# One gathered tile of field 23 in each quad, fetched row by row from ScalarE's queue

## The reference

```python
emb = jax.vmap(lambda tbl, idx: tbl[idx], in_axes=(0, 1), out_axes=1)(embed_tables, sparse)   # [2048, 26, 32]
bi = emb[:, FIRST, :] * emb[:, SECOND, :]                      # the 325 pairs of fields
a = jax.nn.relu(jnp.einsum('bpd,dh->bph', bi, att_w_w) + att_w_b)
scores = jnp.einsum('bph,ho->bpo', a, att_d_w) + att_d_b
att_weight = jax.nn.softmax(scores, axis=1)
att_out = jnp.sum(att_weight * bi, axis=1)
x = jnp.concatenate([att_out, dense], axis=-1)
out = jax.nn.sigmoid(x @ fin_w + fin_b)
```

## Time and profile before

| | |
|---|---|
| median of three runs | 483.76 us |
| the profiled execution | 483.39 us |
| its span, first to last instruction | 481.6 us |
| TensorE matmuls, busy | 450.2 us (93%) |
| VectorE, busy | 372.6 us (77%) |
| GpSimd, busy | 347.9 us (72%) |
| ScalarE, busy | 95.8 us (20%) |

### The profile page before, as it was taken

One profiled execution on the slowest core, in us unless ns is written; L12 is line 12 of the kernel. 1 busy time (PEld: TensorE's weight loads), 2 busy tenths in 40 slices (PEclk: granted clock), 3 DMA queues, 4 the chain that ended last, 5 costly groups with the idle time before them and its releaser, 6 DMA issues.

```text
span 481.6 us, 6198 instructions
## 1 busy us (share of the span) xinstructions
PE 450.2 (93%) x2280; PEld 177.6 (37%) x2280; DVE 372.6 (77%) x645; ACT 95.8 (20%) x198; POOL 347.9 (72%) x372
## 2 busy tenths in 40 slices
PE   0699999999998999999999899999999899999884
PEld 0354443343333533333333443333334344333221
DVE  6337788796965979799775969879786788887985
ACT  0000101131252011112243101113234201114253
POOL 5777777777777777777777777777777777777740
PEclk9999999999999999999999999999999999999998
DMA  6933743121122223222112222213111222322210
GB/s 221 250 13 15 147 58 36 13 15 13 15 13 15 14 14 79 15 14 14 14 14 13 15 13 15 13 13 15 14 13 16 14 15 13 15 13 14 15 10 1
DMA packets 13661, 15.06 MB, mean 31 GB/s; under 512 B 6368, under 2 KB 12608, under 8 KB 13248
## 3 DMA queue, kind: packets, MB, share of 16 engines
q0 software_dynamic: 11776, 6.05, 23.1%
q1 hardware_dynamic: 1360, 7.53, 4.2%
q10 hardware_dynamic: 496, 1.09, 0.6%
HBM read 14.61 MB, written 0.03 MB: 30 GB/s over the span
## 4 chain that ended last, share of the span: by engine, by line
PE 78%; POOL 8%; DVE 5%; issue 4%; DMA 3%; ACT 1%; POOLq 0%; DVEq 0%
PE looked_own L391 33%; PE back_s L391 16%; PE first L405 13%; PE sums_f L415 12%; POOL emb L368 8%; PE sums_s L429 3%; DVE onehot L667 2%; DMA chunk_numbers<-index_chunk 1%; DMA emb<-tables,rows 1%; DMA chunk_of<-chunk_numbers 1%; PE back_f L442 1%; PE back_s L452 1%; DVE look_masked L678 1%; DMA par<-params 1%; DVE ring L691 0%
## 5 line engine op out<-in xcount | busy, mean ns | idle before, releaser
L368 POOL DMA_INDIRECT emb<-tables,rows x324 | 305.9, 944 | 98.7 <-issue 96.9
L691 DVE TENSOR_TENSOR ring<-emb_t,turned 128x512 f32<-128x512 f32 (+9 forms) x180 | 193.9, 1114 | 3.4
L391 PE MATMUL looked_own<-look_table,onehot 128*128 128x448 f32 x434 | 178.0, 554 | 17.0 <-DVE onehot L667 16.7
L391 PEld LDWEIGHTS looked_own<-look_table,onehot 128*128 128x128 f32 x434 | 79.5, 192 | 114.4 <-issue 114.4
L507 ACT ACTIVATE hidden<-first,par 128x512 f32<-128x512 f32 (+1 forms) x84 | 56.5, 678 | 284.7 <-PE first L405 284.4
L391 PE MATMUL back_s<-look_table,onehot 128*128 128x448 f32 x238 | 94.4, 545 | 3.1 <-DVE score L739 3.1
L405 PE MATMUL first<-ring,par 128*32 128x512 f32 (+1 forms) x672 | 90.7, 591 | 4.3 <-DVE ring L691 4.3
L415 PE MATMUL sums_f<-ring,par 128*32 128x512 f32 (+1 forms) x672 | 90.0, 583 | 0.0
L667 DVE TENSOR_TENSOR onehot<-chunk_of,turned 128x2048 f32<-128x2048 f32 (+1 forms) x24 | 48.3, 2018 | 26.6 <-PE looked_own L391 21.2
L391 PEld LDWEIGHTS back_s<-look_table,onehot 128*128 128x128 f32 x238 | 44.0, 190 | 51.7 <-issue 51.7
L368 POOL DMA_INDIRECT emb<-tables,rows_first x44 | 41.8, 950 | 17.2 <-issue 13.1
(11 more groups left out here) (56 smaller groups left out, 101.0 us busy)
## 6 DMA issues: line engine op xcount, KB each, us to landing
emb<-tables,rows POOLq DMA_INDIRECT x324, 3.2
look_table<-tables SPq DMA_DIRECT2D x3, 1568.0 KB, 8.2
chunk_of<-chunk_numbers SPq DMA_DIRECT2D x3, 768.0 KB, 4.9
chunk_of<-chunk_numbers ACTq DMA_DIRECT2D x1, 768.0 KB, 3.8
emb<-tables,rows_first POOLq DMA_INDIRECT x44, 3.8
par<-params ACTq DMA_DIRECT2D x1, 258.5 KB, 3.1
ids<-sparse SPq DMA_DIRECT2D x1, 208.0 KB, 2.5
feats<-dense SPq DMA_DIRECT2D x1, 104.0 KB, 8.1
```

The source lines that it names most:

```text
L368: pool.indirect_dma_start(emb[:, f, g * D:(g + 1) * D], None, stacked, bass.IndirectOffsetOnAxis(ap=row, axis=0),).then_inc(gathered[f], 16)
L391: mm = nc.tensor.matmul(looked_rows[look_bank[tile]], onehot[:, c, g * P:(g + 1) * P], look_table[:, n, c, :], start=c == 0, stop=c == CHU ...
L691: nc.vector.tensor_tensor(slot[:, at:at + n, :], emb_t[:, i:i + n, :], turned[:, f % 2, :].unsqueeze(1).broadcast_to((P, n, P)), ALU.mult) ...
```

## The change

In each quad GpSimd no longer gathers tile 3 of field 23. ScalarE fetches its 128 rows with 128 DMAs of one row (32 floats, 128 bytes) each, straight to their partitions. The table row's number comes from a register; sixteen numbers are loaded to registers at a time, out of a small tile `row_numbers` in SBUF that VectorE makes at the start. Eight rows are issued ahead of the relus of each of sixteen fields: 1 to 9, 12 to 15, 18, 19 and 20. The first of a quad waits until VectorE has transposed field 23 of the quad before. VectorE waits for all 128 rows before it transposes field 23. SP loads the ids of these rows ahead of the first look-up table.

```diff
+ROW_FIELD = 23
+ROWS_LOADED = 16
+ROWS_BESIDE = 8
+ROWS_BESIDE_FIELDS = (*range(1, 10), *range(12, 16), 18, 19, 20)
...
-        return G
+        return G - 1 if f == ROW_FIELD else G
...
+        row_ids = sb("row_ids", [QUADS, P], i32)
+        row_numbers = sb("row_numbers", [QUADS, P], i32)
...
+            sp.dma_start(row_ids[:], row_index).then_inc(row_ids_in, 16)
             load_table(0)
...
+                def fetch_rows(f):
+                    at = ROWS_BESIDE_FIELDS.index(f) * ROWS_BESIDE
+                    if at == 0 and q == 0:
+                        act.wait_ge(row_numbers_ready, 1)
+                    if at == 0 and q:
+                        act.wait_ge(transposed, (q - 1) * F + ROW_FIELD + 1)
+                    if at % ROWS_LOADED == 0:
+                        _, numbers[:] = nc.values_load_multi_w_load_instructions(
+                            row_numbers[q:q + 1, at:at + ROWS_LOADED], engines=(mybir.EngineType.Activation,), min_val=0,
+                            max_val=F * V - 1, skip_runtime_bounds_check_because="rows are clamped to their table")
+                    for p in range(at, at + ROWS_BESIDE):
+                        act.dma_start(emb[p:p + 1, ROW_FIELD, (G - 1) * D:], stacked[bass.ds(numbers[p % ROWS_LOADED], 1), :]
+                                      ).then_inc(rows_fetched, 16)
+
+                numbers = []
+                stacked = tables.rearrange("f v d -> (f v) d")
                 for f in range(1, F):
+                    if f in ROWS_BESIDE_FIELDS:
+                        fetch_rows(f)
                     done = groups_of(f)
...
+            dve.wait_ge(row_ids_in, 16)
+            nc.vector.tensor_scalar(row_clamped, row_ids[:], float(-V), float(V - 1), ALU.max, ALU.min
+                                    ).then_inc(row_steps, 1)
+            dve.wait_ge(row_steps, 1)
+            nc.vector.tensor_scalar(row_wrap, row_clamped, 0.0, float(V), ALU.is_lt, ALU.mult).then_inc(row_steps, 1)
+            dve.wait_ge(row_steps, 2)
+            nc.vector.scalar_tensor_tensor(row_numbers[:], row_clamped, float(ROW_FIELD * V), row_wrap, ALU.add, ALU.add
+                                           ).then_inc(row_numbers_ready, 1)
...
                     if gathers_of(f):
                         dve.wait_ge(gathered[f], (q + 1) * (16 * gathers_of(f)))
+                    if f == ROW_FIELD:
+                        dve.wait_ge(rows_fetched, (q + 1) * (16 * P))
```

More of the change, by code:

```diff
@@ L36, in layout, with attention_fm @@
     return cols, at
-def attention_fm(nc, dense, sparse, tables, params, look_index, chunk_numbers, out):
+def attention_fm(nc, dense, sparse, tables, params, look_index, row_index, chunk_numbers, out):
     f32, i32 = mybir.dt.float32, mybir.dt.int32
@@ L118, in gathers_of @@
             return G - LOOK_TILES[LOOK.index(f)]
-        return G
+        return G - 1 if f == ROW_FIELD else G
+    assert ROW_FIELD not in LOOK and ROWS_BESIDE * len(ROWS_BESIDE_FIELDS) == P and ROWS_LOADED % ROWS_BESIDE == 0
+    assert ROWS_BESIDE_FIELDS[-1] < ROW_FIELD
     assert G * D == P and B % (P * G) == 0 and RING < GROUPS and 1 < END_GROUPS
@@ L211, in attention_fm @@
             "p (t f) -> p t f", f=F) for i in range(2))
+        row_clamped, row_wrap = (final[0:QUADS].rearrange("p g e -> p (g e)")[:, i * P:(i + 1) * P] for i in range(2))
         neg_max = sb("neg_max", [P, G])
@@ L251, in attention_fm @@
         rows_ready = sem("rows_ready")
+        row_ids_in = sem("row_ids_in")
+        row_steps = sem("row_steps")
+        row_numbers_ready = sem("row_numbers_ready")
+        rows_fetched = sem("rows_fetched")
         gathered = [sem(f"gathered{f}") for f in range(F)]
@@ L834 @@
             by_block[:, list(LOOK)].reshape(P, -1, G, len(LOOK)).transpose(1, 3, 2, 0).reshape(-1, P)),
+        "row_index": np.ascontiguousarray(by_block[:, ROW_FIELD].reshape(P, -1, G)[:, :, G - 1].T),
     }
```

## The result

The changed kernel takes 489.13 us, the median of four runs (488.80 to 490.17), against 483.76 before. The medians differ by 5.4 us. The ratio of the runs is 1.0117, with a 95% interval of 1.0102 to 1.0132: slower. The forecast was 485.9. The profiled execution took 488.8 us, its span is 487.0, so 5.4 more than before.

A forecast was written before the change was run, and what follows sets the result against it. TensorE bounds up to quad 2's end, 113.3 us a quad; quad 3 ends 2.1 us later through late relus, three regained waits included: 483.39 + 2.1 = 485.5, plus 0.37 gives 485.9; range 484.7 to 487.2, 8 in 10 up to 502.

The forecast's parts named there:

- The clock was granted at 1.00, 1.00 and 0.98 of full speed and plays no part: TensorE's clock in quads 1, 2 and the last stretch: taken as near full, no time counted for it.
- The cost at the start: SP's extra load and VectorE's small operations ahead of the onehots: nothing, hidden by 1.72 us idle; otherwise 0.8 us.
- the sum against one execution: End 2.1 us later than the profiled execution's 483.39, so 485.5; the runs' median lies 0.37 higher, so 485.9.
- three waits for gathers: VectorE before fields 23, 24 and 25 of quad 3: 0.66, 0.78 and 0.36 us, at most 1.80 us to regain.
- Relu 11 and the score products 5.94 us late: Quad 3, fields 18 to 20: 24 rows delay relu 11 to 455.91, score products 5.94 us late, end 2.1 later.
- the 2.77 us of the three waits: TensorE in quad 3: idle for VectorE's ring 0.88, 1.62 and 0.27 us, to be regained from the 5.94.
- c = 0.47: ScalarE's cost per row in us: issue 0.44 plus 0.03 for register loads; bounds 0.34 and 0.62.
- Issues don't run ahead of a waiting relu: ScalarE: row issues behind a waiting relu wait with it and overlap only with the relu that is running.
- the prediction's limit of 0.52: Fields 1 to 8 of quads 1 to 3: 64 rows and a relu stay hidden up to 0.52 us a row.
- rival B: Rows free, at 0.31 us or less or issued ahead of waiting relus: 482.0 us; chance 0.25 together with D.
- The table load: ScalarE's load at 57.89, when TensorE's first product ended, though idle before: evidence that issues wait behind a waiting relu.
- Rival D: Time goes by GpSimd's gathers: 5.0 us faster, 478.8; given almost nothing, within 0.25 together with B.

The follow-up runs named there:

- filler_3_and_2: Changed kernel plus three and two unused matmuls before and behind the `first` of group 12 of quad 3, where TensorE waits: 486.64 us, ratio 1.0045.
- load_per_8: Changed kernel with sixteen numbers loaded to registers before each eight rows instead of before each sixteen: 509.8 us, ratio 1.0531 to before.
- load_last_only: Kernel before plus only the load of row_ids, behind the first table and the features on SP, its rows unused: 484.48 us, ratio 0.9998.
- rows_12_to_18: Changed kernel with rows beside fields 12 to 18 instead of 12 to 15 and 18 to 20, and row_ids loaded late: 484.84 us, ratio 0.9994.

## Why the prediction was wrong, step by step

The direction and the path of the late relus were right, and the size was short by 489.13 - 485.9 = 3.2 us. Between the two profiles 2.1 us were forecast and 5.4 measured. Of the 3.3 that are missing the clock is 2.4 and the start 1.7, both of which the sum had at nothing, and the late relus came out 0.8 smaller than forecast.

**"The clock was granted at 1.00, 1.00 and 0.98 of full speed and plays no part": the step that failed, and the largest error.** It held in the trace of before, and I carried it over a change that makes TensorE idle. Waits of 2.80 and 2.05 us with one burst between were followed by 1.2 GHz, 2.4 us of the tail (after against filler_3_and_2).

**The cost at the start is "nothing", and the sum against one execution: wrong.** The idle time before the onehots did hide VectorE's three small operations. But the profiled execution of before is one of the earlier starters. I saw its three waits for gathers as 1.80 us that the change could give back. They are also the cover for a start that scatters, and the change removes that cover. The profile after started 1.68 us later, and this time all of it reached the end. In medians, removing the gathers is worth between nothing and 2.1 us (ratios 0.9957 to 1.0 of the five kernels without quad 3's rows and with that stream shorter), not a firm 1.80. Why the changed kernel starts late so often stays open, as said above.

**Relu 11 and the score products 5.94 us late: right.** 457.71 - 449.97 less 1.68 is 6.06. What came after, clock aside, was a little less than forecast: tail 340.7 - 339.4 = 1.3 instead of 2.1. TensorE got more back than the 2.77 us of the three waits: from the score products to the copy of bank 1 it is 464.34 - 449.97 = 14.37 before and 10.77 in filler_3_and_2, so 3.60. In sum 1.3 + 2.4 + 1.7 = 5.4, the whole difference of the two profiles.

**c = 0.47: right, in part by luck.** From the last copy of scores (445.61) to relu 11 (456.97) it is 11.36 us, and 24 x 0.47 = 11.28 were forecast. The two prices in it were both off. From the relu at 449.04 to the one at 453.76 are a register load and eight rows, 4.72 us; from there to 456.97 eight rows alone, 3.21. So the load of sixteen numbers costs 1.51, of which 1.28 lie ahead of the first row: rows follow the start of a relu after 1.42 with it (450.46 - 449.04) and after 0.14 without. I had its price at 0.44, and the issue at 0.44 where the trace shows

```profile
13.47 2.49 ACTq L571 DMA_DIRECT2D emb<-tables  x6
...
13.47 3.66 ACTq L571 DMA_DIRECT2D emb<-tables  x9
```

(3.66 - 2.49) / 3 = 0.39. The two errors cancelled: 0.39 + 1.51 / 16 = 0.48. The 200 ns a register for loads from HBM, which the prediction took from the Trainium skill, "Runtime: NRT & Kernel Launch", Instruction fetch mechanics, are no guide to numbers in SBUF, where it is 1.51 / 16 = 0.09 us here.

**Issues don't run ahead of a waiting relu: right, though the evidence was poor.** In quad 0 of after, where ScalarE idled:

```profile
36.24 1.28 ACT L522 ACT_TABLE_LOAD   x1 [36.24 <-issue]
...
79.32 0.69 ACT L522 ACTIVATE hidden<-first,par 128x512 f32<-128x512 f32 x1 [4.37 <-PE first L420]
79.45 0.63 ACTq L571 DMA_DIRECT2D emb<-tables  x2
```

The rows, with no register load ahead of them, went out 0.13 us after the relu had started, though it had waited 4.37. That refutes rival B's path in this kernel. The Trainium skill, "Perfetto Trace Analysis", has it in its section on DVE / Act instructions that the sequencer goes on while an instruction waits in a queue of its own, and these rows did not go on. But the program writes each relu's wait as a statement of its own (`act.wait_ge`, ahead of the activation), and no run here shows whether it is this separate wait that holds the rows back, so the trace doesn't decide about a wait that belongs to the relu itself. The table load, on which I had rested this, tells nothing: it went ahead of its relu here, at 36.24, right behind the rows, while the first relu came at 59.52, and in the trace of before it started at 57.89 with the end of TensorE's product.

**Quads 0 to 2 hide the rows: right.** 113.32 a quad, as before. load_per_8, whose rows were expected at 0.59 each, shows that this stops somewhere above the 0.48 of the changed kernel; the prediction's limit of 0.52 itself was not tested. Rival D (the time goes by the gathers) is refuted as a gain of 5 us, since no version got below a tail of 337.5. What is true of it is that in the kernel before the gathers do set the end of quad 3 when the start is early, as load_last_only shows.

## What to carry to other kernels

A wait seen in one profiled execution can be the slack that absorbs what scatters ahead of it: before counting it as a gain, ask what varies from run to run and who hides it, and compare tails beside totals. Small jobs on an idle engine are free only where nothing behind them in that engine's order is tight; look for the densest stretch (here the last quad, where the filling work is gone), and place them by it. When a change makes TensorE idle for microseconds in a row, price the slower clock behind the wait too, since here it cost nearly as much (2.4 us) as the wait itself (3.2).

## What the runs showed of the hardware

- A DMA of one row with its address from a register is issued from ScalarE every 0.39 us. Loading sixteen registers from SBUF costs 1.5 us, of which 1.28 pass before the first row. The flight of the rows did not show in the time: at field 23 of quad 3 VectorE waited 0.15 us for them, ahead of a longer wait for the scores.
- The first DMA round trip to memory and back scatters by some 3 us between executions: the two transfers took 4.09 + 3.76 us in one profile (load_last_only), 4.84 + 6.14 in another (rows_12_to_18).
- The granted clock fell to 0.50 after TensorE had idled 2.80 us and during the 2.05 us behind it (after), after 2.40 us (load_last_only), 2.88 us (rows_12_to_18) and 3.55 us (load_per_8), and didn't in quad 3 of the trace of before, whose longest wait there is 1.62. It came back while TensorE worked at the low level: after, 0.98 in 462.4 to 465.0.
- Idle waits filled with matmuls kept the clock at 1.00, but each filler took 0.75 to 0.79 us in line, so that eleven of them cost more than the clock (a tail of 344.5 against 343.1), and five less (340.7).
